# A perceiver block on one core: the first attention's first pass with fixed PSUM banks, another order of turns, and its values in their own chunk

## What is computed

```python
q = (x @ Wq + bq).reshape(B, N, 16, 16)
k = (y @ Wk + bk).reshape(B, M, 16, 16)
v = (y @ Wv + bv).reshape(B, M, 16, 16)
scores = jnp.einsum('bnhd,bmhd->bhnm', q, k) / 4
attn = softmax(scores, axis=-1)
out = jnp.einsum('bhnm,bmhd->bnhd', attn, v)
```

## Time and profile before

| | us |
|---|---|
| median of 3 runs | 1428.24 (1427.45 to 1428.49) |
| profiled execution, its own time | 1428.51 |
| its span in the trace | 1426.8 |
| first pass of layer 0, to the end of its last values turn | 0 to about 214.8 |
| PE busy over the span | 1349.3 (95%) |
| DVE busy | 1106.5 (78%) |
| ACT busy | 1073.0 (75%) |

### The profile page before, as it was taken

The page is one execution under the profiler, slowest core; times in us unless marked ns, Lnnn a source line. Parts: engine busy times, 40 slices in busy tenths (PEclk is TensorE's granted clock), DMA queues, the critical chain, the costliest instruction groups (busy, mean ns, idle before and its releaser), DMA issues.

```text
span 1426.8 us, 37912 instructions
## 1 busy us (share of the span) xinstructions
PE 1349.3 (95%) x15595; PEld 896.8 (63%) x15595; DVE 1106.5 (78%) x1672; ACT 1073.0 (75%) x1596; POOL 198.5 (14%) x196
## 2 busy tenths in 40 slices
PE   5888889999999899999999989999999999999988
PEld 2445455666777596333333347777777777777768
DVE  5677678999100676999999998888888988888864
ACT  3666665666899365888878878888888888888841
POOL 6333210000000004100000000000000004441640
PEclk9999999999999999999999999999999999999999
DMA  4457539555663674556655567777777799898920
GB/s 146 169 199 238 181 147 240 134 138 131 156 177 93 230 248 155 189 188 214 229 190 188 189 162 150 146 146 146 148 145 147 145 184 180 182 190 177 224 78 5
DMA packets 137137, 240.00 MB, mean 168 GB/s; under 512 B 10412, under 2 KB 120710, under 8 KB 136966
## 3 DMA queue, kind: packets, MB, share of 16 engines
q1 hardware_dynamic: 136966, 237.58, 63.0%
HBM read 159.30 MB, written 78.23 MB: 166 GB/s over the span
## 4 chain that ended last, share of the span: by engine, by line
PE 85%; DVE 7%; ACT 3%; issue 3%; POOL 1%; DMA 0%; SPq 0%; POOLq 0%; DVEq 0%; ACTq 0%
PE ps L863 84%; DVE W L1637 2%; ACT W L1407 2%; DVE W L1607 1%; DVE p L1607 1%; DVE q_all L1607 1%; DMA W<-in_ctx_dram 0%; PE ps L902 0%; DVE q_all L1949 0%; POOL q_all L783 0%; ACT p L1383 0%; ACT ps L1383 0%; DVE small L1604 0%; DVE v L1607 0%; DVE small L1944 0%
## 5 line engine op out<-in xcount | busy, mean ns | idle before, releaser
L1607 DVE TENSOR_TENSOR p<-ps,p 128x512 f16<-128x512 f32 (+1 forms) x467 | 350.4, 751 | 60.0 <-ACT ps L1383 57.8
L1383 ACT ACTIVATE p<-ps 128x512 f16<-128x512 f32 (+1 forms) x490 | 329.5, 683 | 83.7 <-PE ps L863 82.5
L863 PEld LDWEIGHTS ps<-q_all,W 128*128 128x128 f16 (+1 forms) x3544 | 229.9, 98 | 67.0 <-issue 5.3
L863 PE MATMUL ps<-q_all,W 128*128 128x128 f16 (+2 forms) x3544 | 264.8, 225 | 4.7 <-DVE p L1607 3.1
L1383 ACT ACTIVATE ps<-ps 128x512 f32<-128x512 f32 x392 | 236.0, 602 | 0.0
L863 PE MATMUL ps<-v,p 128*128 128x130 f16 x3136 | 170.0, 206 | 3.5 <-DVE p L1607 1.9
L863 PE MATMUL ps<-wv,ctxT_a_hi 128*128 128x512 f16 (+1 forms) x588 | 155.0, 345 | 12.5 <-DVE W L1637 10.0
L863 PEld LDWEIGHTS ps<-v,p 128*128 128x128 f16 x3136 | 149.6, 97 | 4.9 <-issue 2.6
L1607 DVE TENSOR_TENSOR v<-ps,v 128x512 f16<-128x512 f32 x196 | 135.4, 691 | 9.5 <-ACT v L1481 3.4
L863 PE MATMUL ps<-wv,ctxT_b 128*128 128x512 f16 (+1 forms) x504 | 136.8, 340 | 0.0
L1720 DVE TENSOR_REDUCE W<-ps 128x1 f32<-128x448 f32 x224 | 124.9, 616 | 11.5 <-PE ps L863 11.5
(11 more groups left out here) (286 smaller groups left out, 2033.2 us busy)
## 6 DMA issues: line engine op xcount, KB each, us to landing
W<-keys_hi SPq DMA_DIRECT2D x54, 896.0 KB, 8.3
W<-keys_low SPq DMA_DIRECT2D x27, 896.0 KB, 11.3
keys_hi<-p SPq DMA_DIRECT2D x75, 224.0 KB, 1.9
keys_low<-p SPq DMA_DIRECT2D x75, 224.0 KB, 1.9
keys_hi<-W SPq DMA_DIRECT2D x65, 224.0 KB, 2.1
keys_low<-W SPq DMA_DIRECT2D x65, 224.0 KB, 1.9
W<-values SPq DMA_DIRECT2D x28, 484.0 KB, 4.1
W<-in_L_ffn_W_dram SPq DMA_DIRECT2D x10, 1024.0 KB, 10.7
```

Of the source, the lines that this page charges most:

```text
L863: return pe.matmul(out_, lhsT, rhs, start=start, stop=stop, **kw)
L1383: return act.activation(out_, in_, ACT.Exp, scale=scale)
L1607: return dve.tensor_tensor(out_, a, b, op)
```

## The change

It touches the first pass of layer 0 alone (layer 1's keeps its banks and order).

1. **Banks** (`banks_of0`). Keys always take banks 0 and 1; scored heads that ACT copies 2 and 3, those that DVE reduces 4 and 5; `ab` takes 6 (`hi`) and 7 (`b`); `lo` and the values take 6 and 7 in turn, one bank each. The queries are projected into bank 5 instead of 7.
2. **Order** (`ORDER0`). The chunk starts with a pair, and `keys1` stands behind `ab`. The `b` part is turned ahead of `hi`, each with its own semaphore, and `hi` waits for its bank only where it starts.
3. **Values** belong to their own chunk; the tiles are dealt 2, 2, 1, 2 instead of 2, 2, 2, 1. The loop ends with the 14th chunk.
4. **Lags**. `low_after` is 2 instead of 1. ACT casts the chunk after next at `lo` instead of at `ab`; DVE's splits of chunks 2 and 3 come behind the `b` copy.
5. **Start**. POOL does the value weights ahead of placing the queries. DVE reads both halves of the queries out of PSUM at once (`read_q0`), places the first half with chunk 0 and the second with chunk 1 (`place_q0(g)`); their scratch moves from `spare` to `att`.
6. **End**. SP stores a chunk's values in its own round of the loop, the last ones thus ahead of the four groups of keys. `run_on` writes bank 1.

```diff
-        L0.low_after, L1.low_after = 1, 2
+        L0.low_after, L1.low_after = 2, 2
-        ORDER0 = "keys1 pair ab values lo pair values pair values keys0 pair values".split()
+        ORDER0 = "pair ab keys1 pair lo values pair values values pair keys0 values".split()
-            for c in range(NCH + 1):
+            for c in range(NCH):
-                    elif kind == "values" and c:
-                        turns.append(("values", c - 1, u))
+                    elif kind == "values":
+                        turns.append(("values", c, u))
-                if L is L0:
-                    pair = i % 4
+        def banks_of0():
+
+            places, before, last, n_one = [], [], {}, 0
+            for i, (kind, n, h) in enumerate(TURNS[0]):
+                if kind == "max":
+                    own = (4, 5) if is_direct(L0, h) else (2, 3)
+                elif kind == "keys":
+                    own = 0, 1
+                elif kind == "ab":
+                    own, n_one = (6, 7), 0
                 else:
+                    own, n_one = (6 + n_one % 2,), n_one + 1
+                places.append(own[0])
+                before.append([(last[bank], bank) for bank in own if bank in last])
-        VPARTS = ((0, 2), (2, 4), (4, 6), (6, CH))
+        VPARTS = ((0, 2), (2, 4), (4, 5), (5, CH))
-                if c:
-                    store_values(c - 1)
+                store_values(c)
...
-            store_values(NCH - 1)
...
                 pe.wait_ge(ctx_split, c + 1)
-                for t in range(CH):
-                    pe.transpose(hi[:, t * P:(t + 1) * P], c16[:, t, 0:P], ident16[:, :])
                 for t in range(CH):
...
-                ins.then_inc(ab_turned, 1)
+                ins.then_inc(b_turned, 1)
+                for bank_left in hi_left:
+                    pe.wait_ge(*bank_left)
+                for t in range(CH):
+                    ins = pe.transpose(hi[:, t * P:(t + 1) * P], c16[:, t, 0:P], ident16[:, :])
+                ins.then_inc(hi_turned, 1)
...
                     if kind == "ab":
-                        if n + 2 < POOL_SPLITS:
-                            split_chunk(n + 2)
-                        dve.wait_ge(ab_turned, n + 1)
+                        dve.wait_ge(b_turned, n + 1)
...
+                        if 0 < n < POOL_SPLITS - 1:
+                            split_chunk(n + 1)
```

More of the change, by code:

```diff
@@ L351, in part_stores, with turn_left @@
             return [16 * ((last - n) // 3 + 1) for n in range(3)]
[L353 to L356 removed]
+        def turn_left(L, i, bank):
             kind, n, h = TURNS[L.n][i]
             if kind == "ab":
[L359 removed]
+                return [(b_out if bank % 2 else hi_out, n + 1)]
             if kind == "lo":
@@ L771, in gpsimd @@
             pool.wait_ge(bk_made, 1)
+            pool.wait_ge(ld_wv, WV_IN[0])
+            settle(split_weights16(L0.wv, wv16[:, :, 0:256], 256, L0.wv_low[1][CB:P, :]))
+            settle(pool.memset(v_out[:, :, :], 0.0))
+            for g in range(2):
+                ins = pool.memset(v_out[:, g, 0:CH * VT0].rearrange("p (h c) -> p h c", c=VW0)[:, :, L0.dh:VW0], 1.0)
+            ins.then_inc(wv_made, 1)
+            pool.wait_ge(wv_made, 1)
             for g in range(2):
@@ L957, in first_pass @@
                 for i, (kind, n, h) in enumerate(TURNS[L.n]):
-                    slot = PAIR[L.n][i]
-                    for left in turn_left(L, BEFORE[L.n][i]):
-                        pe.wait_ge(*left)
-                    if slot == 3 and BEFORE[L.n][i] is None:
-                        pe.wait_ge(q_low, 4) if L is L1 else pe.wait_ge(q_hi, 2)
+                    bank = BANK[L.n][i]
+                    hi_left = []
+                    for turn, own in BEFORE[L.n][i]:
+                        for left in turn_left(L, turn, own):
+                            if kind == "ab" and own == bank:
+                                hi_left.append(left)
+                            else:
+                                pe.wait_ge(*left)
+                    if L is L1 and bank == 6 and not BEFORE[L.n][i]:
+                        pe.wait_ge(q_low, 4)
                     if kind == "ab":
-                        turn_ab(n, slot)
+                        turn_ab(n, bank, hi_left)
                     elif kind == "lo":
-                        turn_lo(n, slot)
+                        turn_lo(n, bank)
                     elif kind == "keys":
```

144 lines of the change are left out of this document (72 added, 72 removed).

## The result

| | before | after |
|---|---|---|
| median of the runs, us | 1427.85 (1426.51 to 1428.49) | 1402.53 (1399.46 to 1403.28) |
| profiled execution, us | 1428.51 | 1402.49 |
| its span, us | 1426.8 | 1400.8 |
| first scores of the second pass, us | 220.97 | 196.64 |
| from there to the end of the span, us | 1205.8 | 1204.2 |

After to before is 0.982, 95% interval 0.980 to 0.984. The forecast was 1401.5 in a range of 1395 to 1412, so the time came out 1 us above it. The steps are another matter: the part that the change touches gained 24.3 us where the sum said 26.7, and the rest of the span made up for most of it.

The account below looks back on a forecast made before the run. PE's waits for banks still holding keys, emptied by ACT then DVE in series, were taken to bound the first pass. Gains of 24.6 and 2.1 us took 1428.51 to 1401.8, stated as a median of 1401.5, range 1395 to 1412.

Parts of the forecast that it names:

- the sum: First pass: 24.6 us gained up to chunk 13's last pair plus 2.1 at the end, 26.7 in all.
- the second wait that was forecast: Chunk's end: the next first pair waits 0.21 us for ACT's part of `keys0`, starting at 11.91 where values end at 11.70.
- a low-clock stretch: Start of the first pass: one PE stretch at a low granted clock, 1.2 us added.
- the step: End: SP stores the last values before loading keys; first scores 9.0 us behind the last pair, gain 2.1.
- the term that it was taken between: End: bounds on last pair to first scores, 7.9 us with loads hidden, or 10.1; 9.0 was taken.
- POOL in the merge's way: Rival, each of 12 chunks: POOL's split stretches the merge ahead of the third reduction, 0.43 us each, 1406.9; chance 0.19.
- The tie at 6.46: Mid-chunk: DVE's first merge starts at 6.46, about when POOL's reads begin at 6.57; being stretched gives 0.1 to 0.43 wait.
- TensorE's floor: Rival: the `lo` copy comes in time, waits of 0.62 and 0.21 a chunk vanish, 1390 to 1394; chance 0.07.
- A worse start: Rival, start: late value weights, DVE blocked by POOL's copies, or low-clock stretches; up to 15 us, 1406 to 1417; chance 0.07.
- Nothing comes of it: Rival: the first pass ends earlier but the second waits for its keys, 24 us; no change, chance 0.03.
- Slower: Rival: a low-clock stretch in each chunk costs 1.5 to 3 us; at 3 it ends at 1444; chance 0.04.

Follow-up runs that it names:

- e1: The kernel after with the old order of turns, values one chunk late, old tile deal and old lag, keeping the fixed banks and new start; 1442.22 us.
- e2: The kernel after with the ring of four pairs of banks in place of the fixed banks, the new order kept; 1426.85 us.
- e4: The kernel after with the tiles of a chunk's values dealt 2, 2, 2, 1 instead of 2, 2, 1, 2; 1408.93 us.
- e5: The kernel after with `keys1`'s rest issued four turns behind its block instead of two, so DVE copies `lo` first; median 1401.38 us.
- e7: e6 with ACT's cast of the chunk after next ahead of its part of `keys0` instead of at `lo`; median 1398.15 us.
- e10: The kernel after with POOL splitting one tile of each chunk's seven, leaving the tokens' rest wrong for six; 1401.99 us.
- e11: e7 plus e9's store order, chunk 0's `keys0` rest ahead of the first reduction, second query half placed at chunk 0's last key block; median 1393.06 us.
- e8: The kernel after with POOL placing queries ahead of the value weights and DVE placing both query halves with chunk 0, as before; 1414.78 us.
- e9: The kernel after with the last chunk's values stored behind the keys' loads instead of ahead of them; median 1403.73 us.
- e6: e5 with the merge of the second pair's copy issued behind the third pair's reduction on DVE; median 1395.94 us.

## Why the prediction was right, and where it was not

**The bound was read rightly.** The waits for the keys' rest are gone, and the copy of `lo` took their place at the turn and with the length that the working gave: from the chunk's first pair, `keys1` at 1.40 (1.50 said), the copy at 5.91 (5.93), the second values at 6.58 (6.60) after a wait of 0.68 (0.62), `keys0` at 8.81 (8.81). e1 and e2 show that the chunk's gain needs both halves of the change: 14.64 and 13.81 us a chunk for one of them alone, 12.01 for both.

**The chunk took 12.01 to 12.02 instead of 11.91, 1.2 us over eleven chunks.** The term that was short is the last: "ACT's part of `keys0` starts 0.26 behind it and takes 1.05 to PE's release". It takes 1.15. ACT's row for the keys starts at 130.72, 2.05 behind the block as said, and the pair at 131.87. e4 shows that this path binds: there the last turn is 0.55 us shorter and the pair starts at the same distance, 3.20. After also has nearly no slack on the other path: the values behind a key block start 0.14 us late (130.60, where 130.46 would be 1.79 behind the block), a gap the sum had only ahead of pairs. So the second wait that was forecast, 0.21 us, has no row in the list of waits. The sum also gave the third reduction 0.26 us to spare (ends at 8.07, wanted at 8.33). It ends at 8.05, but e5 and e7 show a pair to start 0.26 behind such an end, so there was nothing to spare.

**The start took 0.7 us more than said**, up to chunk 2's first pair (47.67 against 47.0): two chunks 2.4 longer, the first pair 0.5 earlier, and 1.2 for a low clock that wasn't there.

| | said | shown |
|---|---|---|
| first pair | 19.9 | 19.36 |
| chunk 0 | 13.2 | 14.63 |
| chunk 1 | 12.7 | 13.68 |
| a low-clock stretch | 1.2 | none |

Chunk 0 missed a wait: "DVE works on it from -0.01 to 1.14" was worked out for a chunk in the middle. In chunk 0 the first pair's reduction stands ahead of the rest of `keys0` on DVE, because `low_after` is now 2 and no turn of values stands between `keys0` and the pair yet, as it does in every later chunk. The reduction starts at 19.97, the rest at 20.98, and `keys1` waits 1.29. Chunk 1 was sized by the split of chunk 3 at 1.56 us; beside POOL's twelve copies it took 1.91, and the merge behind it 1.03. That is 0.77 of the 1.0 missed; the merge of 0.88 that e10 took to 0.61 is 0.25 more. DVE's timeline of after:

```profile
36.48 1.91 DVE L1629 TENSOR_TENSOR stage<-W,stage 128x1344 f16<-128x1344 f32 x1
38.31 1.03 DVE L1629 TENSOR_TENSOR W<-W,p 128x896 f16<-128x896 f16 x1
```

In e11, with the rest of `keys0` ahead of the reduction, the second pair comes 3.2 us behind the first instead of 4.6, which confirms the cause of the first. The value weights, which the prediction feared might be late, were not waited for; e8 shows what they would have cost.

**The end.** 9.19 against 9.0, with SP's stores ahead of the loads as the step said. e9 shows the term that it was taken between: 7.84 with the loads hidden (7.9 said).

**The sum.** First scores at 196.64 instead of 194.3: last pair 187.45 (185.3 said; 0.7 of it from the start, 1.2 from the chunks, 0.2 from chunk 13) and 0.2 at the end. The gain there is 24.3 us, not 26.7. Against before, 5.4 of it is the earlier first pair, 1.0 chunks 0 and 1, 17.2 the eleven chunks and 1.9 the end, less 1.1 for chunk 13, which now makes its own values. The experiments test the middle and the end; of the 5.4 us at the start they show only that the order of turns carries most of it: with the old order, where `keys1` stands ahead of the first pair, the new start brings 1.3 (e1), with the new order 5.6 (e2), one execution each. The single edits of the start were not taken apart.

That the time was hit to 1 us is luck: 2.3 us too few in the first pass met 1.7 us less in the rest of the span than in the profiled execution of before. Almost all of that is one place. In before's timeline PE stands still for 1.48 us in the middle of 16 equal matmuls late in the span, for nothing that the profile shows ("issue"), and none of the other twelve profiles has such a row anywhere from 200 to 1380 us:

```profile
1208.71 0.61 PE L863 MATMUL ps<-v,p 128*128 128x130 f16 x10 [1.48 <-issue]
```

The forecast had nothing for it. Whether other executions of before have it isn't known, since only one has a trace.

**The rivals.**
- *POOL in the merge's way* fell, and not for the reason given. The prediction said that the median merge is not stretched; in after, two of a chunk's four are, in the nine chunks from 48 to 155 us, at 0.98 and 0.91 us, but behind the reductions whose banks PE needs. (Before had one such merge a chunk, 0.96 at 141.51.) The tie at 6.46 went to DVE: that merge took 0.61 or 0.62 in every one of these chunks. With no slack at the third reduction, a tie that went to POOL would have cost its full length each time; that it never did is not explained by any run. The rows agree with the rule of the Trainium skill ("SBUF — State Buffer", section "Who interferes with whom"), by which a VectorE instruction with two SBUF inputs contends with a GpSimd instruction that reads SBUF: e10 shows that it is GpSimd's split that slows the merges. The price, 0.27 to 0.37 us, is below the 0.67 that one of the split's seven instructions takes there.
- *TensorE's floor.* e11's 1393.06 lies in the 1390 to 1394 that it gave, but by other means: the floor was a chunk of 11.91 less 0.83, 11.1, and the shortest chunk of any run is 11.52. Of e11's 10.9 us ahead of the first scores, 3.6 come from chunks 0 and 1 and 1.3 from the end. Its condition, that `lo` comes in time, was not enough (e5); the merge had to move too (e6).
- *A worse start* came in small: 0.7 us in all, with 2.4 in chunks 0 and 1. *Nothing comes of it* did not come: ahead of the first scores PE waits 1.19 us for keys.
- *Slower* by the clock did not come. The granted clock is 1.00 in the middle of the pass in after. The forecast's single low stretch at the start is not recorded in after, e4, e5, e6 and e10 either; the other seven have one or more.

## What to carry to other kernels

When PSUM banks and order both change, draw the chunk by hand from start to start on PE and on the engine that frees the banks, and do it again for the first two chunks, where other work stands in the queues: the middle was right to 1%, the start was off by 8 to 11% a chunk. Before taking a wait away, list what stands behind it on the engine that ended it: in e5 the wait only moved to the next operation, and it took one more move (e6) to gain anything. And look past the total: a part that came out 2.3 us wrong was hidden by one that nobody had touched. An operation that nobody waits for, such as a merge into a running maximum, belongs behind the one that frees a bank.

## What the runs showed of the hardware

- Two-input VectorE operations beside GpSimd's elementwise work took 0.88 to 1.03 us instead of 0.61, and the 1344-wide split 1.91 instead of 1.55; with GpSimd splitting one tile in seven none of 49 merges took over 0.619 (e10).
- A scored pair that waited for VectorE's reduction started 0.25 to 0.36 us behind the reduction's recorded end (after, e5, e7, e11); values that waited for VectorE's copy started 0.06 behind its end, and a pair that waited for ScalarE's part of the keys 0.14 behind (e4). Sums that put them all at 0.1 were off by 0.2 in e5 and e7.
- TensorE started values 0.14 us later behind a key block than behind a pair, in after, e4 and e6 alike, with nothing to wait for. What does it was not tested.
- The low clock at the start comes and goes between kernels that are alike up to that point: 1.00 in all of 15 to 40 us in after, e4, e5, e6 and e10, but 0.50 from 15 to 25 in e9. It cost 1.6 us in e7 (a key block with its values, 5.33 instead of 3.69).
- The first key block at 15.01 in after ran its two 512-column matmuls in 1.01 us instead of 0.59, while the granted clock of that stretch reads 1.00. The recorded clock and the durations don't agree there, and no run here says why.
- One execution of before has 1.48 us of idle TensorE in a row of equal matmuls, with no wait that the profile shows; twelve other profiles have none between 200 and 1380 us.
